# Cross-attention and FFN on one core: x, attention output and first FFN rows transposed on TensorE instead of by DMA, context and FFN weights loaded earlier

## The reference

```
xn = layernorm(x)
q, k, v = xn @ wq.T, ctx @ wk.T, ctx @ wv.T        # 32 query heads of 32, 8 groups of k and v
p = softmax(where(mask, q k.T / sqrt(32), min))    # 4 query heads share one group
x = x + (p v) @ wo.T
y = layernorm(x)
h1, h2 = split(y @ w12.T + b12)                    # 2 x 1024
out = x + (silu(h1) * h2) @ w3.T + b3
```

## Time and profile before

| | us |
|---|---|
| median of 3 runs (1193.53 to 1198.27) | 1196.81 |
| the profiled execution | 1193.76 |
| its span, first to last instruction | 1191.3 |
| PE busy | 1066.7 |
| DVE busy | 617.8 |
| ACT busy | 434.5 |
| POOL busy | 322.5 |
| mean granted TensorE clock | 0.956 |

### The profile page before, as it was taken

One profiled execution on the slowest core, in us unless ns is written; L12 is line 12 of the kernel. 1 busy time (PEld: TensorE's weight loads), 2 busy tenths in 40 slices (PEclk: granted clock), 3 DMA queues, 4 the chain that ended last, 5 costly groups with the idle time before them and its releaser, 6 DMA issues.

```text
span 1191.3 us, 18812 instructions
## 1 busy us (share of the span) xinstructions
PE 1066.7 (90%) x7633; PEld 629.5 (53%) x7633; DVE 617.8 (52%) x1106; ACT 434.5 (36%) x882; POOL 322.5 (27%) x293
## 2 busy tenths in 40 slices
PE   3794788898898989897888999999999999999998
PEld 2583665765656756666554544444444444444443
DVE  5758768677686776776466733263114411431111
ACT  5666454545554544555345642101110111101100
POOL 0504905013040050130349939712001120003000
PEclk9897889899998999998898999999999999999999
DMA  9567797979989979899698775436002700170001
GB/s 308 218 161 166 146 229 161 236 199 195 246 182 238 230 176 237 176 201 221 149 244 239 132 178 163 159 71 212 1 1 53 230 1 1 36 203 9 1 1 71
DMA packets 277925, 181.08 MB, mean 152 GB/s; under 512 B 239056, under 2 KB 249296, under 8 KB 272976
## 3 DMA queue, kind: packets, MB, share of 16 engines
q1 hardware_dynamic: 277840, 179.89, 60.1%
HBM read 93.87 MB, written 27.26 MB: 102 GB/s over the span
## 4 chain that ended last, share of the span: by engine, by line
PE 58%; DVE 13%; DMA 9%; SPq 7%; issue 6%; POOL 4%; ACT 2%; DVEq 0%; ACTq 0%; POOLq 0%
PE bank_dense L926 55%; DMA arena_rows<-w_t 5%; SPq L448 4%; DVE arena_in L1151 3%; DVE arena_in L1229 2%; DVE arena_attn L1237 1%; POOL arena_in L611 1%; DMA arena_rows<-x 1%; SPq L456 1%; POOL arena_in L607 1%; ACT arena_attn L756 1%; DMA arena_attn<-arena_in 1%; SPq L406 1%; POOL arena_in L609 1%; DVE small L1185 1%
## 5 line engine op out<-in xcount | busy, mean ns | idle before, releaser
L926 PE MATMUL bank_dense<-arena_rows,arena_in 128*128 128x256 f16 (+1 forms) x2304 | 362.1, 319 | 2.7 <-DVE small L1128 2.7
L926 PEld LDWEIGHTS bank_dense<-arena_rows,arena_in 128*128 128x128 f16 x2304 | 232.0, 102 | 118.8 <-DVE arena_in L1156 3.2
L756 ACT ACTIVATE arena_attn<-bank_score,arena_in 128x128 f32<-128x128 f32 x512 | 190.8, 468 | 42.5 <-DVE arena_in L1232 42.4
L621 POOL TENSOR_TENSOR small<-small 128x1 f32<-128x1 f32 x32 | 23.8, 744 | 606.6 <-DVE small L1190 606.6
L926 PE MATMUL bank_dense<-arena_out,arena_attn 128*128 128x512 f16 x768 | 172.2, 382 | 9.5 <-issue 8.3
L926 PE MATMUL bank_dense<-arena_attn,arena_rows 128*128 128x512 f16 x768 | 166.4, 379 | 0.0
L926 PE MATMUL bank_dense<-arena_out,arena_in 128*128 128x512 f16 x768 | 166.1, 379 | 0.1
L1275 DVE SCALAR_TENSOR_TENSOR arena_attn<-bank_dense,small,arena_attn 128x512 f32<-128x512 f32 x32 | 24.0, 750 | 241.1 <-PE bank_dense L926 241.1
L926 PEld LDWEIGHTS bank_dense<-arena_out,arena_attn 128*128 128x128 f16 x768 | 74.2, 98 | 97.7 <-issue 12.7
L926 PEld LDWEIGHTS bank_dense<-arena_out,arena_in 128*128 128x128 f16 x768 | 75.1, 98 | 91.0 <-issue 0.8
L926 PEld LDWEIGHTS bank_dense<-arena_attn,arena_rows 128*128 128x128 f16 x768 | 75.1, 98 | 90.6
(11 more groups left out here) (102 smaller groups left out, 1143.4 us busy)
## 6 DMA issues: line engine op xcount, KB each, us to landing
arena_rows<-x SPq DMA_DIRECT2D x32, 512.0 KB, 4.5
arena_attn<-q_scratch SPq DMA_DIRECT2D x48, 256.0 KB, 4.1
arena_rows<-w_t SPq DMA_DIRECT2D x12, 1024.0 KB, 6.9
arena_in<-ctx_t SPq DMA_DIRECT2D x8, 1024.0 KB, 6.8
q_scratch<-arena_attn SPq DMA_DIRECT2D x16, 512.0 KB, 7.3
x_scratch<-arena_rows SPq DMA_DIRECT2D x16, 512.0 KB, 3.3
arena_out<-x_scratch SPq DMA_DIRECT2D x16, 512.0 KB, 5.9
out<-arena_out SPq DMA_DIRECT2D x16, 512.0 KB, 3.8
```

Of the source, the lines that this page charges most:

```text
L756: ins = act.activation(e[:, g % 2, u, SEQ * j:SEQ * j + SEQ], B_SCORE[g % 2][:, SEQ * h:SEQ * h + SEQ], ACT.Exp, bias=neg_max[:, g % 2, h: ...
L926: ins = pe.matmul(dst, lhs(a, c), rhs(b, c), start=(c == 0 and n == 0), stop=(c == KC - 1 and n == 2))
```

## The change

The x rows, the attention output and the rows of the first FFN block are transposed by PE as float32, through the dense banks: 8 transposes of 128x128 for a tile of x, in two units of one bank each, and 2 for the attention output of a step. ACT and DVE then read PSUM and write the hi and lo pieces straight into the transposed place. The probabilities and the rows of FFN blocks 1 to 3 still go by DMA. The context gets a buffer of its own (where the split x rows were) and is loaded and looked at one block ahead; its split waits only for the last v product of the block before. On POOL the split of ctx comes ahead of the roots. k moves from steps 5, 6 to 3, 4, the last two q products from steps 3, 4 to 5, 6. The looks at w12 and w3 are placed a step earlier, the loads of w12 begin as soon as the wq piece under each has been used, in the order 0, 1, 2, 5, 3, 4.

```diff
-Q_AT = {0: (0, 1), 1: (2, 3), 2: (4, 5), 3: (6,), 4: (7,)}
-O_AT = {3: 0, 4: 1, 5: 2, 6: 3}
-K_AT = {5: 0, 6: 1}
+FIRST_Q = {0: 0, 1: 2, 2: 4}
+FIRST_O = {3: 0, 4: 1, 5: 2, 6: 3}
+SECOND_Q = {0: 1, 1: 3, 2: 5, 5: 6, 6: 7}
+SECOND_K = {3: 0, 4: 1}
...
-    if 1 <= t < NB and s == 2:
-        return f"ctx{t}"
+    if 1 <= t < NB - 1 and s == 7:
+        return f"ctx{t + 1}"
...
+def x_tiles(t, s):
+    if t < NB - 1 and s == LAST:
+        return 2 * t + 2, 2 * t + 3
+    if t == NB - 1 and s == 3:
+        return 2 * NB, None
...
-LOOK_AT = {3: "w{0}", 5: "w3{2}", 7: "w{1}"}
+LOOK_AT = {2: "w{0}", 4: "w3{2}", 6: "w{1}"}
...
 sync:
             def load_ctx(t):
                 if t:
-                    sp.wait_ge(s_dense, done("v", t - 1, 1))
-                sp.dma_start(ctx_in, ctx_t[t]).then_inc(s_ctxload, 16)
+                    sp.wait_ge(s_ctx, 4 * t)
+                sp.dma_start(ctx_next, ctx_t[t]).then_inc(s_ctxload, 16)
...
-            def turn_attn(g):
-                sp.wait_ge(s_alo, g + 1)
...
-            turn_tile(0)
-            turn_tile(1)
             load_ctx(0)
...
             load_tile(3)
+            load_ctx(1)
...
 gpsimd:
-            for t in range(1, NB):
-                if t < NB - 1:
-                    root(2 * t + 2)
-                    root(2 * t + 3)
+            for t in range(1, NB - 1):
                 split_ctx(t)
+                root(2 * t + 2)
+                root(2 * t + 3)
...
 scalar:
+            def x_hi(r, h):
+                act.wait_ge(s_dense, done("x", r, h))
+                act.activation(turned_tile(r)[:, 0, 4 * h:4 * h + 4],
+                               bank("x", r, h)[:, :].rearrange("p (c n) -> p c n", c=4), ACT.Copy).then_inc(s_dhi, 1)
+            def attn_hi(g):
+                act.wait_ge(s_dense, done("a", g))
...
+                act.activation(attn_t[:, g % RING, 0], bank("a", g)[:, 0:AB], ACT.Copy).then_inc(s_dhi, 1)
...
 tensor:
+            def turn_x(r, h):
+                if h == 0:
+                    pe.wait_ge(s_norm, r + 1)
+                dst = begin("x", r, h)
+                for c in range(4):
+                    ins = pe.transpose(dst[:, P * c:P * c + P], row_tile(r)[:, P * (4 * h + c):P * (4 * h + c) + P],
+                                       ident[:, :])
+                ins.then_inc(s_dense, 1)
+            def turn_attn(g):
+                pe.wait_ge(s_avread, g + 1)
+                dst = begin("a", g)
+                for u in range(U):
+                    ins = pe.transpose(dst[:, P * u:P * u + P], attn[:, P * u:P * u + P], ident[:, :])
+                ins.then_inc(s_dense, 1)
...
 vector:
+            def x_lo(r, h):
+                dst = turned_tile(r)
+                dve.wait_ge(s_dhi, hi_count("x", r, h))
+                dve.tensor_tensor(dst[:, 1, 4 * h:4 * h + 4], bank("x", r, h)[:, :].rearrange("p (c n) -> p c n", c=4),
+                                  dst[:, 0, 4 * h:4 * h + 4], ALU.subtract).then_inc(s_dread, 1)
```

More of the change, by code:

```diff
@@ L117, in dense_order @@
+def dense_order():
+    n = [("x", r, h) for r in range(2) for h in range(2)]
+    n += [("turn", "q01"), ("spread", "q01"), ("turn", "q23"), ("q", 0, 0), ("spread", "q23"), ("q", 0, 1),
[3 rows of a table added]
+    n += [("x", r, h) for r in range(2, 4) for h in range(2)] + [("v", 0, 0), ("v", 0, 1)]
     for t in range(1, NB + 1):
         for s in range(STEPS):
[L119 to L123, removed]
@@ L137, in dense_order @@
[L137 to L140, removed]
+            g, name, (tile, tile2) = GROUPS * (t - 1) + s, top_at(t, s), x_tiles(t, s)
+            if name:
+                n.append(("turn", name))
+            if tile is not None:
+                n += [("x", tile, 0), ("x", tile, 1)]
+            if t < NB and s in FIRST_Q:
+                n.append(("q", t, FIRST_Q[s]))
+            elif t >= 2 and s in FIRST_O:
+                n.append(("o", t - 2, FIRST_O[s]))
+            elif t < NB and s == LAST:
+                n.append(("v", t, 0))
@@ new lines, in dense_order @@
+            if name and s in SPREAD_EARLY:
+                n.append(("spread", name))
+            if g >= 3:
+                n.append(("a", g - 3))
+            if tile2 is not None:
+                n += [("x", tile2, 0), ("x", tile2, 1)]
+            if t < NB and s in SECOND_Q:
+                n.append(("q", t, SECOND_Q[s]))
+            elif t < NB and s in SECOND_K:
+                n.append(("k", t, SECOND_K[s]))
+            elif t < NB and s == LAST:
+                n.append(("v", t, 1))
+            elif t == NB and s in H_AT:
+                n += [("h", 0, H_AT[s], k) for k in range(2)]
@@ L141, in dense_order @@
+            if name and s not in SPREAD_EARLY:
+                n.append(("spread", name))
+    for s in (8, 9, 10):
+        n += [("a", NG - 11 + s)] + [("h", 0, H_AT[s], k) for k in range(2)]
     n += [("o", NB - 1, q) for q in range(4)]
@@ L612, in split, with split_in_place @@
                 chain[0] += 2
-            def split_in_place(src, dst, by, buf, ready, before):
-                for i in range(4):
+            def split_in_place(src, dst, by, buf, ready, before, pieces=range(4)):
+                for i in pieces:
                     split(src[:, HALF * i:HALF * i + HALF], dst[:, i, 0].rearrange("p c o -> p (c o)"),
@@ L835, in _ @@
             k_hi(0, 1)
+            for r in range(2, 4):
+                for h in range(2):
+                    x_hi(r, h)
             for k in range(2, 4):
@@ L1055, in _ @@
             q_proj(0, 7)
[L1056 to L1057 removed]
+            turn_top("ctx1", max_count("ctx1"), s_max)
+            k_proj(0, 0)
+            spread_top("ctx1")
+            k_proj(0, 1)
+            for r in range(2, 4):
+                for h in range(2):
+                    turn_x(r, h)
             for u in range(U):
```

460 lines of the change are left out of this document (218 added, 242 removed), and 6 rows, old and new, of the table n.

## The result

The changed kernel takes 1168.91 us (median of 4 runs, 1167.86 to 1170.38), the kernel before 1195.53 beside it: a ratio of 0.977, 95% interval 0.9747 to 0.9792. That is 26.6 us faster. The forecast was 1158.0 in a range of 1138 to 1190. The profiled execution has a span of 1166.3 us, 25.0 less than before, where the sum said 35.9.

The account below looks back on a forecast made before the run. PE was taken as nearest to a bound but held by waits and lowered clock. Waits and clock removed, less added transposes and new waits, summed to -35.9 us: from 1193.76 to 1157.9, said as 1158, range 1138 to 1190.

Parts of the forecast that it names:

- start: Up to 72.36 us: wq wait mostly goes, but added work precedes the first factor; +1 us, bounds -4 and +6.
- block 1: PE's 15.38 us wait on POOL's ctx split goes, DVE limits the block to some 58 from 69.2; -11 us.
- blocks 2 to 6: Waits -40.6, clock -10, 160 transposes +24.0, new wait at step 7 +7.5; sum -19.1 us.
- block 7: Waits of 17.7 and clock 3 go, against 6.0 for 40 transposes and 2 new; -12.7 us.
- block 8 and after: First steps of block 8 +3.5 us, with a wait for tile 19; 16 transposes after, +2.4.
- The price of a transpose: Each of 288 added PE transposes costs 0.15 us, the load as the slower of two overlapped parts.
- The dear rival (0.26): Transpose load and matmul run in sequence, 0.26 us each; +28 us, 1186; chance 0.12.
- The wait at step 7: In blocks 2 to 6, PE's third later unit waits for the first x unit's bank; 1.5 us a block, 7.5 in all.
- Clock: Rival: PE is granted half clock around the transposes; +35 us in 7 blocks, 1193; chance 0.05.
- DVE "counted at nothing": DVE changes by -1.4 us a block and has 20 us of air in a block, so no term was counted.
- The wait at the first hidden unit for tile 19: In block 8, tile 19 must be turned before any hidden unit, with no product ahead; 3 us of wait.
- the bank-ring rival: PE stops in mid-step for DVE's division and pieces with only three banks; 0.8 us a step, +51, 1209; chance 0.11.

Follow-up runs that it names:

- experiment 1: The changed kernel with every PE transpose of x and of the attention output issued twice; 1177.93 us, ratio 0.9845.
- (4): The changed kernel with the attention output turned by DMA as before, x still on PE; 1206.02 us, ratio 1.008.
- (5): Three kernels: the changed one plus unread DMA traffic: transposes SP waits for 1210.76 us, 61 transposes without that wait 1192.51, plain copies 1186.16.
- experiment 2: The changed kernel with k, the last two q products and ctx in the steps of before, POOL's new order kept; 1185.92 us, ratio 0.9903.
- experiment 3: The changed kernel with only k and the last two q products in the steps of before, ctx still early; 1166.36 us, ratio 0.9741.
- experiment 6: The changed kernel with DVE's ten FFN factor operations moved from step 6 to step 5 of block 7; 1163.35 us, ratio 0.9734.
- experiment 7: The changed kernel with the look at ctx1 moved behind the first k products of block 0; 1170.84 us, ratio 0.9788.

## Why the prediction was right

The direction and the bargain, PE work paid for waits, were right; the saving came to 25.0 us of span where the sum had 35.9. That the total is this near is in part luck: the start, block 1 and the part from block 8 on missed by 20.0 us together, and blocks 2 to 6, better than said by 8.2, gave much of that back. Point by point (measured from the stretches above):

| stretch | said | measured |
|---|---|---|
| start | +1 | +4.7 |
| block 1 | -11 | -3.3 |
| blocks 2 to 6 | -19.1 | -27.3 |
| block 7 | -12.7 | -13.6 |
| block 8 and after | +5.9 | +14.5 |
| sum | -35.9 | -25.0 |

**The price of a transpose: right in kind, too high.** It said 0.15. In step 7 of block 2 (PE, then its weight loads):

```profile
206.99 1.03 PE L937 MATMUL bank_dense<-arena_in,arena_rows 128*128 128x128 f32 x8
208.81 0.39 PE L928 MATMUL bank_dense<-arena_in 128*128 128x256 f16 x2 [0.78 <-DVE small L1156]
...
206.88 0.91 PEld L937 LDWEIGHTS bank_dense<-arena_in,arena_rows 128*128 128x128 f32 x8
```

Eight run in 1.03 us; one alone lasts 0.28 from start to end, as in the earlier trace rows, so the other seven follow at (1.03 - 0.28) / 7 = 0.107 us. Loads and matmuls overlap. The 0.145 of the earlier trace rows held the start of the first of two loads (one alone takes 0.18 there, so the second followed by 0.11), and halving it was the mistake; over 288 this is 31 us and not 43. By the section on loading weights of the Trainium skill's "TensorE: Matmul & The Clock Gate", cited in the prediction, 128 columns would load in about 0.107 us, an estimate from the page; the trace now agrees. The dear rival (0.26) falls.

**Blocks 2 to 6: waits nearly right, clock and transposes better than said.** PE's idle time fell by 29.0; the sum had 40.6 less 7.5, 33.1. Its busy time rose by 1.7, where the sum had -10 + 24 = +14. With 160 x 0.107 = 17.1 for transposes, 15.4 us came back as clock. So the better result here is 7 us of cheap transposes and 5 us of clock, less 4 us of waits. The wait at step 7 came, smaller than forecast, 3.9 us in five blocks where it said 7.5, and behind the bank of the ctx maxima (the 0.78 above), not behind the tile's first unit. The waits that went are those named; the DMA share fell from 0.90 to 0.78, where about 0.7 was said.

**Clock.** It stood at 1.00 in blocks 2 to 6 with 32 transposes in each, and with 64 in experiment 1, so this rival falls. The rule that the prediction cites with it from the Trainium skill, section on the PE-mode transpose (transposes do not count as PE activity in the way matmuls do), can be neither seen nor excluded here, since products stand between them everywhere. The 48 products of 6.62 us in the earlier trace rows ran at 0.81 over their length, not at half throughout.

**The queue: right in direction, without a price.** The prediction gave the relief no term of its own and put the named waits first. Three experiments point to it as the main cause. With the attention output back in the queue (4) all of the gain is gone; with idle bytes in its place (5) most of it is; and with ctx and k in the steps of before (2) blocks 2 to 6 keep 21.7 of their 27.3 us. What the earlier looks and POOL's new order share in those 21.7 is not told apart. That k comes earlier, named first for the scores' wait, is worth nothing (experiment 3). Late ctx costs 16 to 19 us (experiment 2 against the changed kernel and against 3), mostly in block 7, but under the new order on POOL; what the earlier ctx alone brought stays open.

**DVE "counted at nothing": this failed, and made most of the misses in block 1 and from block 8 on.** The sum counted DVE's work at nothing and had no wait for its division, now in PE's own order. In block 1 it allowed 58 us with DVE at 0.88; measured 65.9 with DVE at 0.71 (46.86 of 65.85). Two of PE's four waits there for a division:

```profile
100.77 0.44 PE L945 MATMUL bank_dense<-arena_in 128*128 128x128 f32 x2 [2.94 <-DVE arena_in L1279]
109.95 0.69 PE L945 MATMUL bank_dense<-arena_in 128*128 128x128 f32 x2 [4.64 <-DVE arena_in L1279]
```

L945 is `turn_attn`, L1279 DVE's `divide`. Behind the first stands a late load after all, behind the second DVE's own list:

```profile
98.09 1.29 DVE L1213 BATCH_NORM_STATS2 small<-arena_rows 128x6 f32<-128x512 f32 x2 [3.19 <-DMA arena_rows<-x]
```

Where a step has few products ahead of its second unit, PE comes to the transpose at once, and must wait for a division that DVE makes late. A DMA transpose had kept this out of PE's order. The same pair costs 9.4 us from block 8 on, and with it most of that part is explained: PE's idle time there rose from 5.7 to 15.1 us, and its busy time by 5.1 (30 transposes make 3.2). The wait at the first hidden unit for tile 19, which the sum had at 3 us, did not come; the 4.53 behind the FFN factors, one step ahead of it, did, and experiment 6 took it away. This is the mechanism of the bank-ring rival (PE stops in mid-step for the division) at two fifths of its price: all waits at L945 for a division in the whole run make 20.3 us, not 51.

**Start.** The direction and the named wait were right (4.92 where it said 2.3), but it was not the cause: removing it gave 1 us at most (experiment 7). What holds the stacks stays open.

## What to carry to other kernels

When one engine issues all transfers from one list, a small transfer can cost more than its bytes (here 5% of them cost 18 to 24 us): look for what lands late for the engines that wait in order behind it, and ask of each named wait of the bound engine what its releaser had waited for. Work moved onto the bound engine is nearly free while it falls into waits (288 transposes more for 9 us), but its place then ties that engine to another one's order; look at the steps that have nothing else ahead of it (first block, last block). Move one load a step earlier, or ten small operations out of the way, before building anything larger: here that gave 13 us for a few moved lines.

## What the runs showed of the hardware

- A float32 transpose of 128x128 on PE costs 0.107 us back to back at a granted clock of 1.00, 0.27 us for one alone.
- Issuing one DMA transpose of 16 tiles takes SP from 1.3 to 7.3 us (median 1.97 over the 64 of the changed kernel, 2.89 before); one of 4 tiles at least 1.19. SP's time is itself a resource. The issues of the changed kernel (shortest, median and longest in ns):

```profile
L454 SPq DMA_TRANSPOSE arena_attn<-arena_attn x64: 1317/1969/7045, 88.2 to 670.8; - x64
```

Those of before, first the probabilities, then the attention output:

```profile
L448 SPq DMA_TRANSPOSE arena_attn<-arena_attn x64: 1317/2892/7315, 83.1 to 702.3; - x64
...
L456 SPq DMA_TRANSPOSE arena_attn<-arena_in x64: 1189/1262/2144, 101.2 to 724.7; - x64
```

The 64 issues for the attention output alone took SP some 81 us before (64 x 1.26); the landings of the earlier trace rows come on top.
